# Graph layer keys from high and low parts: six float32r products in place of two float32 products, and ScalarE's forty-column copy dropped

## The reference, cut to what matters

```python
self_feat = vcq @ W_self.T + b_self                    # (32, 128, 128)
for d in range(2):
    kv = self_feat[:, :20]                             # NONGT = 20 neighbours
    qh = (self_feat @ Wq[d].T + bq[d]).reshape(B, N, 16, 8)
    kh = (kv @ Wk[d].T + bk[d]).reshape(B, 20, 16, 8)
    aff = einsum('bnhd,bmhd->bnhm', qh, kh) / sqrt(8)
    # mask, label bias, softmax over the 20, weighted sum of kv, output product
```

## Time and profile before

| | us |
|---|---|
| median of 3 runs | 592.37 |
| lowest, highest | 592.29, 592.44 |
| the profiled execution, its own time | 591.88 |
| its span, first to last instruction | 590.3 |
| TensorE busy in the span | 580.5 |
| VectorE, ScalarE, GpSimd busy | 510.7, 474.8, 292.0 |
| one step of the graph layer | 8.16 |

### The profile page before, as it was taken

The page is one execution under the profiler, slowest core; times in us unless marked ns, Lnnn a source line. Parts: engine busy times, 40 slices in busy tenths (PEclk is TensorE's granted clock), DMA queues, the critical chain, the costliest instruction groups (busy, mean ns, idle before and its releaser), DMA issues.

```text
span 590.3 us, 17418 instructions
## 1 busy us (share of the span) xinstructions
PE 580.5 (98%) x5600; PEld 535.3 (91%) x5600; DVE 510.7 (87%) x1117; ACT 474.8 (80%) x1733; POOL 292.0 (49%) x352
## 2 busy tenths in 40 slices
PE   8999999999999999999999999999999999999997
PEld 8889899999999999999999999989988899999996
DVE  6899988998898889889888888888886989888896
ACT  4888889789879897898798888978887777777773
POOL 3447535354354354453543553656654565555652
PEclk9999999999999999999999999999999999999999
DMA  7310210201202102112021031023353433443321
GB/s 236 95 42 1 59 40 23 58 16 41 57 0 57 44 13 57 33 24 57 2 56 48 9 108 44 18 72 99 110 150 93 110 103 100 120 117 106 100 75 48
DMA packets 63428, 38.99 MB, mean 66 GB/s; under 512 B 19630, under 2 KB 61214, under 8 KB 63390
## 3 DMA queue, kind: packets, MB, share of 16 engines
q1 hardware_dynamic: 61758, 34.29, 21.7%
q0 software_dynamic: 1632, 4.21, 2.2%
HBM read 30.73 MB, written 7.76 MB: 65 GB/s over the span
## 4 chain that ended last, share of the span: by engine, by line
PE 91%; DVE 5%; ACT 2%; issue 1%; DMA 0%; DVEq 0%
PE banks L751 10%; PE banks L721 10%; PE banks L734 9%; PE banks L2155 7%; PE banks L689 5%; PE banks L693 5%; PE banks L690 5%; PE banks L1521 4%; PE banks L2123 4%; PE banks L2137 4%; PE banks L774 3%; PE banks L775 2%; PE banks L776 2%; PE banks L705 2%; PE banks L706 2%; PE banks L707 2%
## 5 line engine op out<-in xcount | busy, mean ns | idle before, releaser
L610 POOL TENSOR_TENSOR late_blocks<-late_blocks,p_rsum 128x512 f32<-128x512 f32 x96 | 99.0, 1052 | 156.9 <-DVE p_rsum L1096 156.9
L948 ACT ACTIVATE late_blocks<-banks,neg_max 128x128 f32<-128x128 f32 x384 | 137.1, 402 | 27.9 <-DVE neg_max L1090 27.9
L948 ACT ACTIVATION_READ_ACCUMULATOR late_blocks<-banks,neg_max 128x1 f32 x384 | 93.1, 243 | 0.0
L929 ACT ACTIVATE wide<-banks 128x512 f32<-128x512 f32 x124 | 75.5, 609 | 4.5 <-PE banks L693 3.3
L689 PE MATMUL banks<-xT_hi,w_qkv_hi 128*128 128x256 f32 x256 | 77.6, 303 | 0.0
L1090 DVE TENSOR_REDUCE neg_max<-banks 128x8 f32<-128x1024 f32 x64 | 76.4, 1193 | 1.3 <-PE banks L721 1.3
L693 PE MATMUL banks<-xT_hi,w_qkv_lo 128*128 128x256 f32 x256 | 72.0, 281 | 0.0
L690 PE MATMUL banks<-xT_lo,w_qkv_hi 128*128 128x256 f32 x256 | 71.8, 280 | 0.0
L721 PE MATMUL banks<-wide 64*128 64x128 f32 x1024 | 66.0, 278 | 0.2
L721 PEld LDWEIGHTS banks<-wide 64*128 64x128 f32 x1024 | 59.8, 188 | 6.1 <-issue 3.7
L948 ACT ACTIVATE third_p<-banks,neg_max 128x128 f32<-128x128 f32 x128 | 47.0, 387 | 21.1 <-DVE neg_max L1090 21.1
(11 more groups left out here) (187 smaller groups left out, 1700.3 us busy)
## 6 DMA issues: line engine op xcount, KB each, us to landing
g_v_block<-v_image SPq DMA_DIRECT2D x16, 303.8 KB, 3.5
early<-in_mask SPq DMA_DIRECT2D x16, 220.0 KB
early<-in_mask SPq DMA_DIRECT2D x80, 44.0 KB
x_in<-in_x SPq DMA_DIRECT2D x16, 128.0 KB, 2.1
x_res<-in_x SPq DMA_DIRECT2D x16, 128.0 KB, 2.2
x_scratch<-x SPq DMA_DIRECT2D x16, 128.0 KB, 1.9
f_x_in<-x_scratch SPq DMA_DIRECT2D x16, 128.0 KB, 2.4
f_x_res<-x_scratch POOLq DMA_DIRECT2D x16, 128.0 KB, 2.8
```

What stands on the lines that cost most here:

```text
L610: pool.tensor_tensor(p[:, heads, :], p[:, heads, :], p_rsum[:, b, heads].unsqueeze(2).broadcast_to([128, 4, T]), ALU.mult).then_inc(p_read ...
L929: act.activation(qk_dst(name) if name[0] == "q" else v_dst(name), work_ps[bank], ACT.Copy).then_inc(bank_free[bank], 1)
L948: act.activation(p[:, m, :], s_ps[b][:, e, j, :], ACT.Exp, bias=neg_max[:, b, 4 * e + j:4 * e + j + 1], accum_out=p_sum[:, b, m:m + 1]).th ...
```

## The change

The weights that are split now hold the keys' two matrices as well: `wq_hi` and `wq_lo` have four slices where they had two, and GpSimd's two instructions of `split_weights` go over 512 columns in place of 256. `keys` multiplies the first forty columns of `selfT_hi` and `selfT_lo` by these parts, three float32r products for each direction, as queries and values do. ScalarE's second instruction and the tile `kvT` are gone, and VectorE's split waits for the first one. `keys` waits for VectorE's `selfT_split` in place of ScalarE's `kv_saved`. The low by low product is left out, as it is in queries and values.

```diff
@@ split_weights (GpSimd)
-        hi, lo, raw = ((wq_hi, wq_lo, g.gqk_w[:, 0:2, :]),
+        hi, lo, raw = ((wq_hi, wq_lo, g.gqk_w[:]),
@@ keys (TensorE)
-            pe.wait_ge(kv_saved, s.n + 1)
+            if at(s, 0):
+                pe.wait_ge(weights_split, 2)
+            pe.wait_ge(selfT_split, s.n + 1)
...
             for d in range(2):
-                last = pe.matmul(k_ps(s)[:, d * BM:d * BM + BM], g.gqk_w[:, 2 + d, :],
-                                 kvT[:], start=True, stop=True)
+                dst, near = k_ps(s)[:, d * BM:d * BM + BM], slice(0, 2 * NG)
+                pe.matmul(dst, wq_hi[:, 2 + d, :], selfT_hi[:, near], start=True, stop=False)
+                pe.matmul(dst, wq_lo[:, 2 + d, :], selfT_hi[:, near], start=False, stop=False)
+                last = pe.matmul(dst, wq_hi[:, 2 + d, :], selfT_lo[:, near], start=False, stop=True)
@@ save_selfT (ScalarE)
-            act.activation(selfT_hi[:], turns_ps[:, 0:2 * T], ACT.Identity, bias=g.b_selfT[:])
-            act.activation(kvT[:], turns_ps[:, 0:2 * NG], ACT.Identity, bias=g.b_selfT[:]).then_inc(kv_saved, 1)
+            act.activation(selfT_hi[:], turns_ps[:, 0:2 * T], ACT.Identity, bias=g.b_selfT[:]).then_inc(selfT_high, 1)
@@ split_selfT (VectorE)
-            dve.wait_ge(kv_saved, s.n + 1)
+            dve.wait_ge(selfT_high, s.n + 1)
```

More of the change, by code:

```diff
@@ L1804, in graph_phase @@
     selfT_hi, selfT_lo = (sb(f"g_selfT_{n}", [128, 2 * T], F32R) for n in ("hi", "lo"))
-    wq_hi, wq_lo = (sb(f"g_wq_{n}", [128, 2, D], F32R) for n in ("hi", "lo"))
+    wq_hi, wq_lo = (sb(f"g_wq_{n}", [128, 4, D], F32R) for n in ("hi", "lo"))
     wo_hi, wo_lo = (sb(f"g_wo_{n}", [128, 2 * HC * GCH * GD], F32R) for n in ("hi", "lo"))
@@ L1811, in graph_phase @@
     k_block = g.late_blocks[:, 0:8 * HALF * NG].rearrange("p (s b d h m) -> p s b d h m", s=2, b=2, d=2, h=HALF)
-    kvT = sb("g_kvT", [128, 2 * NG])
     v_rows = sb("g_v_rows", [BM, HC, 2, GCH, GW])
@@ L1839, in graph_phase @@
     self_b_ready = sem("g_self_b_ready")
-    kv_saved = sem("g_kv_saved")
     v_image_cleared = sem("g_v_image_cleared")
@@ L1846, in graph_phase @@
     selfT_full = sem("g_selfT_full")
-    selfT_split = sem("g_selfT_split")
+    selfT_high, selfT_split = sem("g_selfT_high"), sem("g_selfT_split")
     weights_high, weights_split = sem("g_weights_high"), sem("g_weights_split")
```

## The result

The changed kernel took **596.82 us**, median of 6 runs (595.80 to 597.82), beside 592.33 us for the kernel before (median of 6, 591.61 to 592.83). The ratio is 1.0079 with a 95% interval of 1.007 to 1.0089: 0.8% slower. The profiled execution of after has a time of its own of 597.05 us and a span of 594.3 us, against 591.88 and 590.3. So the span grew by 4.0 us; the rest of the 5.2 lies outside it, and comes back at the end of this text.

What follows compares the result with a forecast made beforehand. The prediction took TensorE's stream to bound every graph step: 15 pairs x 0.22 = 3.30 us and 0.42 for pair 0 made +3.72, so 596.1 us against the median of 592.37, range 595.1 to 597.3.

Steps and rivals of the forecast that it cites:

- TensorE is the bound of the graph steps: Graph layer: TensorE's stream is busy all 8.16 us of a step, so whatever is added to it adds to the time.
- A narrow pair costs 0.11: Keys on TensorE: each weight load and narrow product takes 0.11 us; two more pairs add 0.22 us a pair of sequences.
- the one odd spacing of before: Keys' four loads before: the first, behind a 288-column product, was given 0.13 us, the other three 0.113 each.
- What hides it, nothing: Steady graph steps: queries and weighted sum follow keys at once, so nothing hides the +0.22 us; the keys' consumers are off the path.
- ScalarE's copy, worth 0: Graph steps: dropping ScalarE's 16 instructions gives back 0, as ScalarE idles 2.07 us a step; far bound 2.4 us.
- Rival 3: Graph steps: an earlier VectorE split closes part of TensorE's 0.17 us gaps, down to +1.3 us and 593.7; chance 7%.
- 0.07 us of slack: Before the input transposes: TensorE could follow VectorE's split at 504.41, but its load starts at 504.48, so VectorE does not cause the gap.
- 16 x 0.30 = 4.8 less: ScalarE's busy time: 16 instructions go, 0.30 us each as at pair 0, so it falls by 4.8 us or a little less.
- Pair 0, +0.42: First pair: keys wait for VectorE's split and start at 448.16 for 447.89; with six pairs of 0.11, queries come 0.42 us later.
- GpSimd, 0: Weight split before the attention phase: doubled columns delay a normalisation chain by 0 to 0.53 us; taken as 0.
- rival 1: Keys on TensorE: narrow float32r pairs are cheap, under 0.075 us each, so the change is faster, 591.1 us; chance 5%.
- Rival 2: Keys on TensorE: a narrow float32r product is handled as a float32 one, twelve pairs for four, +14.3 and 606.7 us; chance 5%.

Runs made afterwards that it cites:

- high_only_late_queries: Changed kernel with only the high by high product for the keys, and queries put behind the weighted sum in TensorE's order; 607.73 us, ratio 1.0264.
- two_small_loads: Kernel before with two narrow float32r products added ahead of the keys' float32 ones, each loading 40 columns of weights; 595.05 us, ratio 1.0043.
- early_high: Changed kernel, keys waiting for ScalarE's selfT_high first and for VectorE's selfT_split only before the third product; 596.16 us, ratio 1.0065.

## Why the prediction was right

The prediction was 596.1 us, slower, for 596.82 measured. Its own sum was made for the profiled execution: 3.72 us of span. The span grew by 4.0, and 3.89 of it lies in the graph steps. The mechanism held; two terms were sized a little low, and one argument on the way did not carry what was put on it.

- **TensorE is the bound of the graph steps: shown.** Two products alone gave 8.39 for 8.16, four in place of six gave 8.16 again, and the edits that left TensorE's products alone (the wait, GpSimd's part, the copy, the wait put off behind two products) left the steady step alone. The bound has a limit below: with two or three products the step is 8.06, and ScalarE's copy of the transposed input sets it.
- **A narrow pair costs 0.11, in either type: shown.** Predicted +0.22 a step, measured 0.23 on average over the twelve steady ones, and 3.38 for 3.30 over the 15 pairs behind the first. The keys to queries distance of 0.66 to 0.69 came out at 0.69: five spacings of 0.11 and one of 0.14, right behind the values. The prediction took 0.13 for the one odd spacing of before, which it read from the last load of the values to the first of the keys; that spacing is still there, and the odd one among the keys' own loads is 0.14. With it before's other three come to 0.11 instead of 0.113.
- **What hides it, nothing; and no consumer of the keys became late: shown in after's trace.** The exponential on ScalarE ends at 508.30 + 0.74 = 509.04, 2.08 us behind the keys' start (2.14 before), and the transposes that need it start 0.59 later. The two rows in after's timeline of the same step:

```profile
508.30 0.74 ACT L2250 ACTIVATE late_weights<-late_weights 128x640 f32<-128x640 f32 x1
...
509.63 0.70 PEld L2139 LDWEIGHTS banks<-ident,late_weights 128*120 128x120 f32 x6
```

- **ScalarE's copy, worth 0: shown** by the kernel that keeps it. Rival 3 asked that part of the 0.17 us gaps closes, and each is still 0.17 with the split 0.19 us further ahead. Before the run this was less sure than the prediction had it. Its 0.07 us of slack rests on TensorE following VectorE by 0.05; with the 0.12 of pair 0 the slack is nothing, and the gap would be VectorE's. Nor were the gaps in two places only, both behind the scores: the third stands in front of the scores. What makes them no run tells. The step that failed is the figure for ScalarE's busy time: 16 x 0.30 = 4.8 less was forecast, and 2.0 came with the copy as the only difference (1.2 between the two pages). The step multiplied recorded durations, and these overlap, at pair 0 by 0.12.
- **Pair 0, +0.42: mis-sized.** It was 0.51, in both traces of the changed kernel. The forecast let TensorE follow VectorE by 0.05 us, from a load behind VectorE at pair 1. At this place it was 0.12, in the changed kernel and in the one with the wait alone, and the prediction's own rows had it: the keys stood 0.12 behind ScalarE's copy at this very place before. The keys were forecast at 448.16, and at 448.36 stand 0.20 later; 0.13 of that came before it (ScalarE's rounding starts at 447.25 for 447.12) and 0.07 this delay. The other 0.02 of the 0.09 is not placed.
- **GpSimd, 0: right.** The 0.77 us more did not fit into 0.61 of idle time, and the next instruction came 0.18 later; the attention phase absorbed that. The kernel with this part alone was 1.0000 (0.9991 to 1.0009).
- **Rivals 1 and 2 fall.** The turning point of rival 1 was 0.075 us a pair; it is 0.11. The Trainium skill, "TensorE: Matmul & The Clock Gate", section "Weight-path perf modes", switches the fast load on for 128 weights of any type but FP32. With 192 ns a load, and 8.16 us for four float32r products as for four float32 records, this case shows nothing of it for float32r. Rival 2 would have brought 12 records, and 6 came.
- **The rest, 0.7 us of the median.** 0.17 of it are the two terms above, 0.08 and 0.09. Some 0.4 is time outside the span; the prediction took the 1.58 us of before as given, and the six runs of after have a median of 2.0. What is left, 0.1, is less than one kernel's spans differ (589.6 to 591.4 us for the kernel before).

**What stays open.** The time outside the span was 1.5 to 1.7 us in every run of before, of the kernels with the wait or GpSimd's part alone, of those with two to four products for the keys, and of the one with 44 products at the end. In the kernels with six products for the keys, or with two added to before's, it was 2.2 to 2.8 us in one to three runs of each (three of six of the changed kernel, the profiled one among them: 597.05 - 594.3 = 2.75). A longer graph layer alone is not the cause, since high_only_late_queries is 11 us longer still and had 1.5 to 1.6; nor are more instructions at TensorE's end. What the kernels that show it have in common is six records for a pair of sequences where the keys stand, but no run tells whether these bring it about, or how, or why only some executions have it.

## What to carry to other kernels

Where one engine is busy without a gap, price a change by the records that it adds to that engine, not by the work that it takes from others: here 16 instructions less on ScalarE were worth 0.14 us, and 32 records more on TensorE cost 3.6. Count records and not products: a float32 product is two and one split into high and low parts is three, so here, with 40 moving columns and full weight loads setting the pace, the split only costs. And before taking work away from such an engine, look for the shortest chain through the others beside it; here it lay 0.10 us below, and two records less than before gave half of their 0.22 us.

## What the runs showed of the hardware

- A float32r product with 128 weight columns and 40 moving ones is one record, paced by 0.11 us, just as one of the two records of a float32 product (step 8.16 us with four of either, 8.39 with six); the load is recorded with 190 to 192 ns for both types.
- Behind a weight load of 40 columns the next load starts 0.04 us later where it stands among narrow products, and 0.13 to 0.14 where it stands behind one that moves 288 columns (two_small_loads).
- TensorE starts 0.12 us behind the end of what it waits for where the keys open pair 0, be it VectorE (448.24 to 448.36, 448.09 to 448.21) or ScalarE (447.77 to 447.89), and 0.05 behind VectorE in another place (452.91 to 452.96). In early_high, with two of the keys' products ahead of the wait, it is 0.06 at pair 0 too (449.13 to 449.19). Why was not tried.
- ScalarE's records overlap by some 0.12 us: 16 instructions with 0.29 each, 4.6 us, were worth 2.0 us of busy time.
- TensorE's weight loads stand idle in three places of a graph step, 0.17, 0.17 and 0.19 us. The changed kernel has all three unchanged, put down to no engine. What makes them is open.
